# Splitting the next batch's queries during attention, and tanh at the border of two pairs

## The reference

```python
q = (x @ Wq.T + bq)...   # 16 heads of 16 dims; k and v likewise
sim = einsum('bhid,bhjd->bhij', q, k) / sqrt(16) / (abs(temperature) + 0.1)
for fi, freq in enumerate([31., 37., 41., 43., 47.]):
    scores = scores + alpha[h, fi] * sin(2*pi * sim / freq + phi[h, fi])
w = sigmoid(scores);  w = w / (sum(w) + 1e-10)
out = w @ v              # then @ Wo.T + bo, layer norm
```

## Time and profile before

| | us |
|---|---|
| median of 3 runs | 7117.2 (7109.4 to 7120.61) |
| the profiled execution | 7119.98 |
| its span | 7118.2 |
| first stage, to the end of its stores | 412.6 |
| from there to the first sine | 62.7 |
| first sine to last tanh | 5743.1 |
| rest | 899.8 |

### The profile page before, as it was taken

One profiled execution on the slowest core, in us unless ns is written; L12 is line 12 of the kernel. 1 busy time (PEld: TensorE's weight loads), 2 busy tenths in 40 slices (PEclk: granted clock), 3 DMA queues, 4 the chain that ended last, 5 costly groups with the idle time before them and its releaser, 6 DMA issues. The chain is left out here.

```text
span 7118.2 us, 130314 instructions
## 1 busy us (share of the span) xinstructions
PE 6113.5 (86%) x48057; PEld 4363.9 (61%) x48057; DVE 5773.2 (81%) x4353; ACT 5853.0 (82%) x5874; POOL 205.8 (3%) x217
## 2 busy tenths in 40 slices
PE   6539999999999999999999999999999999826555
PEld 3326666666666666666666666666666666625444
DVE  6648888888888888888888888888888888857775
ACT  1139999999999999999999999999999999901111
POOL 0000000000000000000000000000000000010000
PEclk8769999999999999999999999999999999966666
DMA  7931111111111111111111111111111111131220
GB/s 291 358 143 47 47 47 46 46 47 46 45 47 45 45 47 47 47 46 47 46 47 46 47 47 46 47 45 46 47 45 46 47 45 47 30 81 46 50 52 20
DMA packets 322961, 446.10 MB, mean 63 GB/s; under 512 B 158980, under 2 KB 189604, under 8 KB 321384
## 3 DMA queue, kind: packets, MB, share of 16 engines
q1 hardware_dynamic: 317032, 432.81, 19.4%
q0 software_dynamic: 5376, 5.30, 0.3%
HBM read 284.11 MB, written 153.75 MB: 62 GB/s over the span
## 5 line engine op out<-in xcount | busy, mean ns | idle before, releaser
L593 ACT ACTIVATE a_wave<-a_ps_turn 128x1024 f32<-128x1024 f32 x5120 | 4915.0, 1365 | 132.2 <-PE a_ps_turn L527 131.9
L527 PE MATMUL a_ps_turn<-a_q_r,a_k_r 64*128 64x512 f32 x20480 | 3392.0, 399 | 399.8 <-ACT a_wave L593 249.3
L609 DVE SCALAR_TENSOR_TENSOR a_weight<-a_wave,a_head_c,a_weight 128x2048 f32<-128x2048 f32 x1536 | 3612.6, 2352 | 59.5
L527 PE MATMUL a_ps_turn<-a_q_r,a_rounder 64*128 64x512 f32 x20480 | 3241.4, 392 | 4.6 <-issue 4.6
L527 PEld LDWEIGHTS a_ps_turn<-a_q_r,a_k_r 64*128 64x128 f32 x20480 | 1951.8, 185 | 1574.9 <-ACT a_wave L593 804.5
L527 PEld LDWEIGHTS a_ps_turn<-a_q_r,a_rounder 64*128 64x128 f32 x20480 | 1976.6, 186 | 244.6 <-issue 9.4
L609 DVE SCALAR_TENSOR_TENSOR a_weight<-a_wave,a_head_c 128x2048 f32<-128x2048 f32 x512 | 1203.9, 2351 | 844.4 <-ACT a_wave L593 844.4
L587 ACT ACTIVATE a_weight<-a_weight,a_head_c 128x2048 f32<-128x2048 f32 x512 | 1186.0, 2316 | 5.2 <-DVE a_weight L609 5.2
L547 PE MATMUL a_ps_out<-a_weight,a_v_r 128*32 128x512 f32 x4096 | 547.2, 606 | 7.6 <-ACT a_weight L587 5.4
L506 POOL COPY a_head_c<-a_table 128x5 f32 (+1 forms) x128 | 114.3, 893 | 5596.2 <-ACT a_weight L587 5596.1
L547 PEld LDWEIGHTS a_ps_out<-a_weight,a_v_r 128*32 128x32 f32 x4096 | 80.8, 108 | 194.7 <-issue 184.0
(11 more groups left out here) (231 smaller groups left out, 1919.3 us busy)
## 6 DMA issues: line engine op xcount, KB each, us to landing
q_d<-p_q_hl SPq DMA_DIRECT2D x80, 1024.0 KB, 8.3
a_q_r<-q_d SPq DMA_DIRECT2D x256, 320.0 KB
a_k_r<-k_d SPq DMA_DIRECT2D x512, 128.0 KB
a_q_r<-q_d SPq DMA_DIRECT2D x256, 160.0 KB
k_d<-p_k_hl SPq DMA_DIRECT2D x8, 4096.0 KB, 15.2
a_k_r<-k_d SPq DMA_DIRECT2D x512, 64.0 KB
o_d<-a_out SPq DMA_DIRECT2D x512, 34.0 KB
num<-o_d SPq DMA_DIRECT2D x32, 512.0 KB
```

The source lines that it names most:

```text
L527: last = nc.tensor.matmul(ps_turn[slot_of(r, s, f)][:, half, :], exact(w(rows[half])), exact(q_r[rows[half], k, f, :]), start=(i == 0), st ...
L593: nc.scalar.activation(wave[:, s // 2 % 2, f, s % 2, :], ps_turn[slot_of(r, s, f)][:].rearrange("p a b -> p (a b)"), ACT.Sin, scale=TURN_I ...
L609: return v.scalar_tensor_tensor(both(weight[:, i, :, :]), both(wave[:, i % 2, f, :, :]), head_c[:, k, f:f + 1], to, ALU.mult, ALU.add)
```

## The change

In the first stage only batch 0's q is split there. The drawn q of every batch goes to a new scratch tensor `q_d` as it is (1 MB, `whole_kept`), and batch 0's second half is split behind its k. In attention VectorE splits the q of batch b + 1 while batch b runs: 16 parts of 128 dims x 128 queries, two in each of the heads 1 to 8 of a batch, ahead of the waves of pairs 1 and 3. SyncE loads each part (64 KB) and stores its two halves (320 KB each), and the order in its queue is: the next head's loads, the store of one part, the output's store, the store of the other part, two loads of parts. SyncE and VectorE now run a loop over batches with 16 heads written out in it. On ScalarE tanh moves from between f = 3 and f = 4 of an odd unit to ahead of f = 0 of the next even unit, the border of two pairs; on TensorE the product with V moves from f = 3 to f = 4 of an odd unit.

```diff
@@ project_qkv, SyncE
-                def keep(b):
+                def keep(b, split=False):
+                    sp.wait_ge(q_ready, b + 1)
+                    sp.dma_start(q_d[b, :, :].rearrange("(m p) l -> p m l", p=P), qk_sb[:, 0, :, :]).then_inc(whole_kept, 16)
                     sp.wait_ge(v_ready, b + 2)
                     sp.dma_start(v_d[b, :, :, :], v_sb[:]).then_inc(v_kept, 16)
-                    for m in range(KC):
-                        for f in range(NF):
-                            sp.wait_ge(q_split, NF * (KC * b + m) + f + 1)
-                            sp.dma_start(q_d[b, :, m * P:(m + 1) * P, f, :].rearrange("i p l -> p i l"),
-                                         q_hl[:, f, :, :]).then_inc(q_kept[f], 16)
+                    if split:
+                        for m in range(KC):
+                            for f in range(NF):
+                                sp.wait_ge(q_split, NF * m + f + 1)
+                                sp.dma_start(qs_d[b, :, m * P:(m + 1) * P, f, :].rearrange("i p l -> p i l"),
+                                             q_hl[:, f, :, :]).then_inc(q_kept[f], 16)
@@ project_qkv, VectorE: body(0, True), then the loop with body(b, False)
+                def body(b, split):
                     dve.wait_ge(q_summed, b + 1)
+                    dve.wait_ge(whole_kept, 16 * (b + 1))
...
-                    dve.wait_ge(q_ready, b + 1)
-                    dve.wait_ge(rate_in, 32)
-                    split_q(b, 0)
+                    if split:
+                        dve.wait_ge(q_ready, b + 1)
+                        dve.wait_ge(rate_in, 32)
+                        split_q(0)
...
-                    split_q(b, 1)
...
+                    if split:
+                        split_q(1)
+                        dve.wait_ge(q_split, NF * KC)
@@ oscillatory_attention, SyncE
+                for m in range(KC):
+                    sp.dma_start(rate[:, m, :], ...).then_inc(rate_in, 16)
...
+                def fetch_q(b, n):
+                    wait_pos(sp, q_split, H * b + n - 1)
+                    dims, cols = part_of(n)
+                    sp.dma_start(q_in[:, n % 2, :], q_d[b + 1, dims, cols]).then_inc(q_loaded[n % 2], 16)
+                def keep_q(b, n):
+                    sp.wait_ge(q_split, H * b + n + 1)
+                    dims, cols = part_of(n)
+                    for i in range(2):
+                        sp.dma_start(qs_d[b + 1, i, dims, :, cols], q_hl[:, n % 2, i, :, :]).then_inc(q_kept[n % 2], 16)
...
+                def body(b, j):
+                    ahead = not isinstance(b, int) or b < B - 1
+                    split = ahead and 1 <= j <= H // 2
+                    if ahead and j == H - 1:
+                        for k in range(2):
+                            sp.wait_ge(q_kept[k], 16 * H * (b + 1))
+                    if ahead or b == B - 1 and j < H - 1:
+                        load(b + (j + 1) // H, (j + 1) % H)
+                    if split:
+                        keep_q(b, 2 * j - 2)
+                    if not isinstance(b, int) or b or j:
+                        store(b, j)
+                    if split:
+                        keep_q(b, 2 * j - 1)
+                    if ahead and j < H // 2:
+                        fetch_q(b, 2 * j)
+                        fetch_q(b, 2 * j + 1)
@@ oscillatory_attention, TensorE
-                            if f != NF - 2:
+                            if f != NF - 1:
                                 continue
@@ oscillatory_attention, ScalarE
-                            if f == 4 and s % 2 and (after(g) or s > 1) and (main(g) or s == 1):
-                                p = PAIRS * g + s // 2 - 1
+                            if f == 0 and s % 2 == 0 and (after(g) or s > 2) and (main(g) or s < 4):
+                                p = PAIRS * g + s // 2 - 2
@@ oscillatory_attention, VectorE
+                def split_q(b, n):
+                    k = n % 2
+                    dve.wait_ge(q_loaded[k], 8 * H * b + 16 * (n // 2 + 1))
+                    wait_pos(dve, q_kept[k], 16 * H * b + 32 * (n // 2))
+                    v.tensor_tensor(q_all[:], q_in[:, k, :] broadcast, rate[:, n % KC, :] broadcast, ALU.mult)  # 128 x 640
+                    v.tensor_copy(q_hl[:, k, 0, :, :].bitcast(F32R), q_all[:])
+                    v.tensor_tensor(q_hl[:, k, 1, :, :].bitcast(F32R), q_all[:], q_hl[:, k, 0, :, :], ALU.subtract)
+                for i in range(PAIRS):
+                    if i in (1, 3) and 1 <= j <= H // 2 and (not isinstance(b, int) or b < B - 1):
+                        split_q(b, 2 * j - 2 + i // 2)
```

More of the change, by code:

```diff
@@ L128, in _ @@
                     sp.sem_inc(q_kept[f], 16)
+                sp.sem_inc(whole_kept, 16)
                 sp.sem_inc(k_kept, 16)
@@ L153, in _ @@
                     sp.dma_start(rate[:, m, :], tab_d[8 * m:8 * m + 8, 1, :].unsqueeze(1).broadcast_to([8, HD, NF])).then_inc(rate_in, 16)
-                with sp.Fori(0, B // 2 - 1, 1) as pair:
+                for b in range(2):
+                    sp.wait_ge(x_turned, b + 2)
+                    load(b + 2, b)
+                    keep(b, b == 0)
+                with sp.Fori(1, B // 2 - 1, 1) as pair:
                     for k in range(2):
@@ L164, in _ @@
                 for f in range(NF):
-                    sp.wait_ge(q_kept[f], 16 * (KC * B + 1))
+                    sp.wait_ge(q_kept[f], 16 * (KC + 1))
+                sp.wait_ge(whole_kept, 16 * (B + 1))
                 sp.wait_ge(k_kept, 16 * (B + 1))
@@ L376, in oscillatory_attention @@
         v_r = sb("a_v_r", [P, 2, LT, VP])
+        q_in = sb("a_q_in", [P, 2, QW])
+        q_all = sb("a_q_all", [P, NF, QW])
+        q_hl = sb("a_q_hl", [P, 2, 2, NF, QW])
+        rate = sb("a_rate", [P, KC, NF])
         warm = sb("a_warm", [P, 2])
@@ L412, in heads_in_turn, with heads_by_batch @@
                 body(g, g % 2, g % 3)
+        def heads_by_batch(eng, body):
+            for j in range(H):
+                body(0, j)
+            with eng.Fori(1, B - 1, 1) as b:
+                for j in range(H):
+                    body(b, j)
+            for j in range(H):
+                body(B - 1, j)
+            body(B, 0)
         LOADS = 16 * 14
@@ L446, in _, with load @@
                 sp.wait_ge(phase_kept, 16)
-                def load(g, k):
+                for m in range(KC):
+                    sp.dma_start(rate[:, m, :], tab_d[8 * m:8 * m + 8, 1, :].unsqueeze(1).broadcast_to([8, HD, NF])).then_inc(rate_in, 16)
+                def load(b, j):
+                    g, k = H * b + j, j % 2
                     wait_pos(sp, filled, NF * U * (g - 1))
-                    b, h = g // H, g % H
                     to_q = lambda row, count, src: sp.dma_start(q_r[row:row + count, k, :, :], src).then_inc(qk_loaded[k], 16)
@@ L453, in load @@
                     to_k = lambda row, count, i, src: sp.dma_start(k_r[row:row + count, k, i, :], src).then_inc(qk_loaded[k], 16)
-                    dims, head = bass.ds(h * HD, HD), bass.ds(h, 1)
-                    for j in range(2):
+                    dims = slice(j * HD, (j + 1) * HD)
+                    for n in range(2):
                         for i in range(2):
[L457 to L461, removed]
+                            to_k(64 * n, 2 * HD, i, k_d[b, 2 * i:2 * i + 2, dims, :])
+                            to_k(64 * n + 2 * HD, HD, i, k_d[b, 2 * i, dims, :])
+                        to_q(64 * n, 2 * HD, qs_d[b, 0:1, dims, :, halved(n)].broadcast_to([2, HD, NF, HALF]))
+                        to_q(64 * n + 2 * HD, HD, qs_d[b, 1, dims, :, halved(n)])
+                        to_q(64 * n + 3 * HD, 2, ph_d[:, j:j + 1, :, halved(n)].rearrange("i o f l -> i (o f) l"))
@@ L470, in store @@
                                      out[VP * c:VP * c + VW, 1 - k, :]).then_inc(stored[1 - k], 16)
                 load(0, 0)
-                def body(g, k):
-                    if not isinstance(g, int) or g + 1 < HEADS:
-                        load(g + 1, 1 - k)
-                    if after(g):
-                        store(g, k)
-                heads_of(sp, body)
+                def body(b, j):
[15 more added lines that the diff above has]
+                        fetch_q(b, 2 * j + 1)
@@ L480, in _ @@
+                heads_by_batch(sp, body)
                 for k in range(2):
```

50 lines of the change are left out of this document (33 added, 17 removed).

## The result

| | before | after |
|---|---|---|
| median of 4 runs, us | 7115.2 (7109.4 to 7120.61) | 6984.8 (6984.06 to 6986.03) |
| span of the profiled execution | 7118.2 | 6982.3 |
| first sine of attention at | 475.3 | 335.05 |
| first sine to the start of the last tanh | 5743.1 | 5708.2 |
| start of the last tanh to the end | 899.8 | 939.0 |

The ratio to before is 0.9817, its 95% interval 0.98 to 0.9834. The forecast was 6951 with a range of its own from 6935 to 6975; with rivals B and C the range was 6925 to 6990. So the time lies outside the forecast's own range and inside the wide one. The span came out 30.7 us over the sum of 6951.6, and the table says where: the first stage gave 1.7 us more than forecast (140.3 for 138.6), attention 6.9 more (34.9 for 28), and the third stage, for which no step of the prediction had a price, lost 39.2.

What follows compares the result with a forecast made beforehand. The first stage was taken as bound by DMA of split q, attention by ScalarE. Span 7118.2 - 140 (first stage) + 1.4 (attention's start) - 28 (tanh at jumps) = 6951.6, so 6951 us, own range 6935 to 6975.

Steps and rivals of the forecast that it cites:

- B: Rival: in the first stage a slower chain, 31 to 33 us a batch, gives 6975 us; chance 0.12.
- C: Rival: attention's loop jump gives nothing back, as the product delays the fetch and ScalarE jumps late; 6973 us, chance 0.11.
- First stage, -140: First stage: without seven batches' splits and stores, TensorE's chain sets 28.1 us a batch; -140 us, ends -151 and -120.
- F: Rival: the first stage keeps its period because its chain has another wait the trace hides; 7090 us, chance 0.05.
- Splits, 0: Attention, VectorE: 112 split parts of 2.0 us each fit its idle time and tanh's slack; cost 0.
- D: Rival: split parts in attention cost more than VectorE's room; at 4 us each 7088 us, chance 0.04.
- SyncE's queue, 0: Attention: the next head's loads start 2 to 4 us later behind part stores, within 12 us of slack; cost 0.
- E: Rival: attention's loads come too late behind part stores at about 50 GB/s; 8130 us, chance 0.04.
- tanh at the border, -28: Attention, ScalarE: moved tanh fills the wait for TensorE at 18 loop jumps, 1.55 us each; -28 us, ends -34 and -11.
- 7118.2 - 140 + 1.4 - 28: Whole kernel: span before, first stage, two more loads at attention's start, and tanh at the jumps; 6951.6 us of span.

## Why the prediction came out as it did

- **First stage, -140.** Right, and by its steps: the period 27.73 us (28.1), k's last store issued at 258.01 (259), the stage's end at 270.4 (272.5), the first sine at 335.05 (337). q's matmuls vary most, 8.5 to 10.2 us from batch to batch. That TensorE's chain is next late was argued then and is shown now by the two versions that burden it and the DMA engines. B and F are out.
- **Splits, 0.** About right: a part takes 2.13 us (2.0 taken), both TENSOR_TENSORs 0.82 instead of 0.72 and the copy 0.49 instead of 0.38. Each is 0.1 us longer, the copy too, which has no broadcast operand: the prediction scaled the whole duration by the columns, while 2.29 and 0.82 us for 2048 and 640 columns, and 1.22 and 0.49, each leave about 0.15 us that doesn't scale (my estimate from these rows). The broadcast costs nothing that shows. Steady heads stay at 44.17 us, and the parts cost at most 5 us of attention. D is out.
- **SyncE's queue, 0.** Right. No fill waited for a load behind the first head; the stores of parts landed in 5.1 us. E is out.
- **tanh at the border, -28.** The mechanism was right, the size low. ScalarE's idling at the jumps fell from 77.7 to 44.0 us, 1.9 us at each of the 18, which is the whole length of tanh and the end of -34 where I took 1.55; in the kernel before, the edit by itself gave 36 to 41 us. So the product cost the jump nothing that shows. C is out. How the 44.0 divide was wrong: I had about 50 us of waits for TensorE, and they are 11.6. The rest, 32.4 us, 1.8 at each jump, is ScalarE's own jump, which was to hide inside TensorE's 7.67 us. TensorE's return, which I took as fixed, was mostly no longer the later of the two.
- **The step that failed: "7118.2 - 140 + 1.4 - 28".** It takes the third stage as unchanged because its code is. The missing term was +39 us. That the time still falls within 6925 to 6990 is luck: the range was widened to 6990 for B and C, a slower first stage and a move of tanh that gives nothing, and neither came. The prediction did cite the Trainium skill (Runtime: NRT & Kernel Launch, Instruction fetch mechanics) for TensorE's and ScalarE's jumps and never asked the same of VectorE's, whose code ahead of the third stage grew from 596 records to 2350, as its loop of 2 heads became one of 16. The row to ask from was in the trace of before: a jump over 331 instructions that cost 0.40 us, when that of TensorE cost 2.98. A cheap jump is a matter of place, so it can be lost.

VectorE's small addition is held until GpSimd's add ends, in the changed kernel and in the kernel before with moved code. The Trainium skill (SBUF — State Buffer, SBUF: two separate sides) says that VectorE and GpSimd have one pair of ports in common, which the first to start holds for its whole instruction, and names VectorE operations with two inputs in SBUF among those that want it. The trace agrees for this one, by 4.47 us against 0.17; BATCH_NORM_STATS2, with one input, ran beside the same add at 0.41 us each, as it did alone. A TENSOR_SCALAR of 128x8 with one input (`spread`, L1052 in the kernel before) was held too: it ended at 6463.49, GpSimd's add at 6463.46. The page also names fast modes of VectorE that want the pair; no run here tells which mode it ran in.

## What to carry to other kernels

An edit that adds instructions to an engine moves all code behind it, and a loop there can lose a cheap jump: list for each engine the loops behind the edit and what their jumps cost now, and give that a term. When a stage slows down whose code is unchanged, look at the first instruction behind each jump, and for small operations that take as long as one on another engine. The DMA queues' row of instruction packets tells at once whether a loop fetches its code in every turn. A delay of some us may be absorbed, or may bring two engines together and cost twice its length, so ask what the late engine then runs beside.

## What the runs showed of the hardware

**Where a jump is cheap.** Counting VectorE's records in the traces, each loop body once, the third stage's loop of 331 begins at record 596 in the kernel before and 2350 in the changed one. Modulo 512 the six places are 80, 84 and 210 with a cheap jump (0.4 us of issue, no instruction packets) and 284, 302 and 398 with a dear one (3.0 to 3.6, and at one of the six jumps of each run 4.3 to 4.5; five packets a turn). The Trainium skill (Runtime: NRT & Kernel Launch, Instruction fetch mechanics) speaks of two pages of 256 instructions, outside of which a taken branch stalls. Read as any two adjacent pages, that would make a jump inside them cheap, and a loop of 331 spans three only if it begins at 182 or later in its page; 284 and 398, 114 apart, can't both do so, however the count is shifted. Measured and this reading differ. What fits is a pair of pages with a fixed border every 512, if the true places lie 29 to 80 below the counted ones (or 432 to 483 above, where instructions that leave no record come before). It isn't the only fit. The packets that VectorE's dear loop fetches are of 8192 bytes each, and with a border every 128 the places are 80, 84 and 82 for the cheap jumps and 28, 46 and 14 for the dear ones, so a rule with borders that close fits too. No run here decides between the two, and a loop of another length was not tried.

**The jump's price isn't its cost.** About 3.4 us of issue at each of six jumps cost 39 us with the meeting and about 4 without it.
